# Two attention layers on one core: the order of every engine's steps read from a table instead of made by a list scheduler

## The reference

```python
# layer 0: 64 latents attend to 64 context rows and to themselves, 16 heads of 16
h = concatenate([ctx, x], axis=1)                       # (32, 128, 256)
q = x @ q_w + q_b;  k, v = split(h @ kv_w + kv_b)
attn = softmax(where(mask, q k^T / 16, -inf))            # 64 x 128 per head
r = (attn @ v) @ out_w + out_b + x
r = rmsnorm(r, postnorm_w)
x = gelu(r @ mlp_w1 + mlp_b1) @ mlp_w2 + mlp_b2 + x      # 256 -> 1024 -> 256
# layer 1: 256 columns attend to 256 columns of the context, 8 heads of 64
xn = (x - mean) * rsqrt(var + eps) * gamma + beta        # mean, var of a whole sequence
q = Wq xn + bq;  k, v = split(Wkv ctx + bkv)
att = softmax(q^T k / 8)                                 # 256 x 256 per head
out = x + Wo (att v) + bo
```

## Time and profile before

| | us |
|---|---|
| median of 3 runs | 603.48 |
| lowest, highest | 601.45, 603.9 |
| span of the profiled execution | 602.0 |
| PE busy | 570.4 |
| DVE busy | 547.9 |
| ACT busy | 504.4 |
| POOL busy | 420.8 |

### The profile page before, as it was taken

One profiled execution on the slowest core, in us unless ns is written; L12 is line 12 of the kernel. 1 busy time (PEld: TensorE's weight loads), 2 busy tenths in 40 slices (PEclk: granted clock), 3 DMA queues, 4 the chain that ended last, 5 costly groups with the idle time before them and its releaser, 6 DMA issues.

```text
span 602.0 us, 21122 instructions
## 1 busy us (share of the span) xinstructions
PE 570.4 (95%) x8564; PEld 463.7 (77%) x8564; DVE 547.9 (91%) x1053; ACT 504.4 (84%) x1904; POOL 420.8 (70%) x419
## 2 busy tenths in 40 slices
PE   4799999999999999999999999999999999998976
PEld 4689877777888787887888777887877777876755
DVE  5977889999999999999899989998999999999996
ACT  2848779988899987998899888998989897968873
POOL 2643468777588767796777865886676985787764
PEclk9779999999999999999999999999999999999989
DMA  8213001011102111111111111011111111110110
GB/s 285 76 38 103 22 19 55 20 37 30 35 29 57 43 38 28 38 56 32 33 46 55 38 38 27 31 35 29 37 29 38 32 38 40 37 29 20 40 24 23
DMA packets 50080, 26.45 MB, mean 44 GB/s; under 512 B 38048, under 2 KB 48320, under 8 KB 49984
## 3 DMA queue, kind: packets, MB, share of 16 engines
q1 hardware_dynamic: 49984, 25.11, 15.3%
HBM read 22.99 MB, written 2.10 MB: 42 GB/s over the span
## 4 chain that ended last, share of the span: by engine, by line
PE 64%; DVE 23%; ACT 6%; POOL 4%; DMA 2%; issue 1%; SPq 0%
PE bank L671 60%; DVE E1b L1179 6%; DVE nm L1162 5%; PE bank L792 4%; POOL E1b L1445 3%; ACT E1b L1362 3%; DVE nm L1017 2%; DVE E L1027 2%; DMA mski<-in_msk 1%; DVE QS L1155 1%; ACT E L1259 1%; DVE PT L1035 1%; DVE hm L1099 1%; ACT hm L1333 1%; DVE mrow L989 1%; PE bank L822 1%
## 5 line engine op out<-in xcount | busy, mean ns | idle before, releaser
L1445 POOL TENSOR_TENSOR E1b<-E1b,rs 128x512 f32<-128x512 f32 x255 | 264.0, 1060 | 85.4 <-DVE rs L1168 80.4
L1362 ACT ACTIVATE E1b<-bank,nm 128x256 f32<-128x256 f32 x512 | 237.0, 495 | 28.6 <-DVE nm L1162 28.4
L1162 DVE TENSOR_REDUCE nm<-bank 128x2 f32<-128x512 f32 x256 | 164.2, 674 | 9.4 <-PE bank L671 9.0
L1179 DVE STREAM_TRANSPOSE E1b<-E1b 128x1024 f32<-128x1024 f32 x128 | 155.9, 1227 | 5.7 <-POOL E1b L1445 4.8
L671 PE MATMUL bank<-ctx,QS 64*128 64x256 f32 x1024 | 134.5, 394 | 1.7 <-DVE PT L1035 1.0
L671 PE MATMUL bank<-E1b,CT 32*64 32x256 f32 (+1 forms) x4224 | 120.9, 375 | 10.2 <-ACT E1b L1362 3.6
L671 PEld LDWEIGHTS bank<-E1b,CT 32*64 32x64 f32 x4224 | 95.4, 132 | 30.4 <-ACT E1b L1362 5.1
L1362 ACT ACTIVATION_READ_ACCUMULATOR E1b<-bank,nm 128x1 f32 x512 | 116.7, 228 | 0.0
L671 PEld LDWEIGHTS bank<-ctx,QS 64*128 64x128 f32 x1024 | 91.6, 186 | 25.5 <-issue 6.8
L1259 ACT ACTIVATE E<-bank,nm 128x128 f32<-128x128 f32 x256 | 90.7, 409 | 9.6 <-DVE nm L1017 9.6
L1259 ACT ACTIVATION_READ_ACCUMULATOR E<-bank,nm 128x1 f32 x256 | 63.8, 249 | 0.0
(11 more groups left out here) (119 smaller groups left out, 823.1 us busy)
## 6 DMA issues: line engine op xcount, KB each, us to landing
CT<-in_hT SPq DMA_DIRECT2D x256, 32.0 KB, 1.9
hraw<-in_hT SPq DMA_DIRECT2D x8, 512.0 KB, 3.4
ctx<-in_ctx SPq DMA_DIRECT2D x32, 128.0 KB, 2.7
xnat<-in_xn SPq DMA_DIRECT2D x8, 256.0 KB, 2.8
E1b<-in_w SPq DMA_DIRECT2D x2, 1024.0 KB, 8.8
out<-y SPq DMA_DIRECT2D x16, 128.0 KB, 1.7
E1b<-in_kvw SPq DMA_DIRECT2D x2, 256.0 KB, 4.6
mski<-in_msk SPq DMA_DIRECT2D x32, 1.0 KB
```

Of the source, the lines that this page charges most:

```text
L1162: e.tensor_reduce(nm1[:, u % 16, :], bank[place["S", u]][:, :].rearrange("p (i t) -> p i t", i=2), AX.X, ALU.max, negate=True).then_inc(dv ...
L1179: e.transpose(E1b[:, k:k + 2, :, :], E1b[:, k:k + 2, :, :]).then_inc(dve_steps, 1)
L1362: t = e.activation(E1b[:, r, i, :], bank[bk][:, i * 256:(i + 1) * 256], ACT.Exp, bias=nm1[:, r, i:i + 1], scale=1.0, accum_out=sum1[:, r, ...
L1445: e.tensor_tensor(E1b[:, u % 16, :, :], E1b[:, u % 16, :, :], rs1[:, u % 16, :].unsqueeze(2).to_broadcast([128, 2, 256]), ALU.mult).then_i ...
```

## The change

`Plan.order()` no longer schedules. A table `ORDER` names for each of the five engines all of its steps in order, and for each PE step that takes banks the banks by number. `order()` reads the table, checks it against `plan()`, derives which step must have emptied a bank before its next use, and walks the lists into one order that respects all dependencies. `COST`, `SHIFT`, `MODE` and the due times are gone. The set of 2505 steps and their dependencies are the same. In the table some steps have another engine than before: of the 64 snp 13 run on DVE and 51 on POOL (22 and 42 before); ze 40 on DVE and 84 on ACT (47 and 77); W1e 18 and 14 (21 and 11); gs 21 and 11 (24 and 8); xn 5 and 11 (9 and 7); te 28 and 36 (27 and 37); Np none on DVE (one before); hhi 8 and none (6 and 2); a few of the weights' preparation the other way. One wait changes with it: q waits for xn and Mg on each engine where one of them runs, since they may now stand on two.

```diff
-ENTER = dict(rows=95, cols=92, rows32=95, cols32=95, grid=95)
-LEAVE = dict(rows=100, cols=162, rows32=100, cols32=140, grid=150)
...
-STAY = dict(full=0, rows=0.6, grid=2, cols=1.5, rows32=1.5, cols32=0)
...
+ORDER = {
...
+xol:1 qe:1:1 X:2 X:3 yy:1 sq:1 X:6 X:7 X:9 X:8 sn:2:0:2 X:1 X:0 sn:2:0:3 N:6 dd:1 X:5 rstd:1 te:2:0:2 X:4 te:2:0:3 N:2
...
     def order(self):
-        engines = ("PE", "DVE", "ACT", "POOL", "SP")
-        free = {e: 0 for e in engines}
-        mode, table = "full", "exp"
-        idle = [(0, b, None) for b in range(8)]
...
+        for step, banks in lists["PE"]:
+            assert len(banks) == len(self.banks[step])
+            for use, b in zip(self.banks[step], banks):
+                self.place[use], self.before[use] = int(b), holds.get(b)
+                holds[b] = self.emptied[use]
+        ahead, over = {e: 0 for e in lists}, set()
+        while len(self.steps) < len(self.todo):
...
                 elif name == "q":
                     p, c = key
                     pa, pb = take_all(("q", 2 * p, c), ("q", 2 * p + 1, c))
-                    w.wait_ge(*last([("xn", p), ("Mg",)]))
+                    for x in lasts([("xn", p), ("Mg",)]):
+                        w.wait_ge(*x)
```

More of the change, by code:

```diff
@@ L252, in order @@
-        self.span = max(over.values())
-        self.over = over
-        self.steps = [s for _, s in sorted(self.steps, key=lambda x: x[0])]
+        lists = {e: [(tuple(int(x) if x.isdigit() else x for x in word.partition("@")[0].split(":")),
+                      word.partition("@")[2]) for word in words.split()] for e, words in ORDER.items()}
+        for e, entries in lists.items():
+            for step, _ in entries:
+                assert e in self.on[step] and step not in self.runs
+                self.runs[step] = e
@@ new lines, in order @@
+        while len(self.steps) < len(self.todo):
+            n = len(self.steps)
+            for e, entries in lists.items():
+                while ahead[e] < len(entries):
+                    step = entries[ahead[e]][0]
+                    if not all(a in over for a in (*self.after[step], *(
+                            self.before[use] for use in self.banks[step] if self.before[use]))):
+                        break
+                    self.steps.append(step)
+                    over.add(step)
+                    ahead[e] += 1
+            assert len(self.steps) > n
@@ L315, in plan @@
                 prev("t", p2, r) for r in range(4)],
-                banks=[("s", g, c, r) for r in range(4)], kind="other")
+                banks=[("s", g, c, r) for r in range(4)])
             for r in range(4):
-                add("smax", g, c, r, on=A, at=at(), after=[("s", g, c), prev("t", p2, r)])
-                add("sexp", g, c, r, on=P, at=at(), after=[("smax", g, c, r), prev("t", p2, r)],
-                    empties=(("s", g, c, r), "other"))
-                add("sn", g, c, r, on=A, at=at(), after=[("sexp", g, c, r)])
@@ L357, in plan @@
+            add("W2", g, c, on=V, after=[("gsp", g, c), ("W2", g, c - 1) if c else None] + [
+                ("w2l", c)], banks=[("W2", g, 0)] if c == 0 else [])
+        add("X1", g, on=A, after=[("W2", g, 3), ("xop", g)] + (
+            [("fin", 2 * (g - 2) + i) for i in range(2)] if g >= 2 else []), empties=("W2", g, 0))
         if g + 1 < NG:
-            add("lx", g + 1, on=D, at=at(), after=[("X1", g)])
-    add("qs", on=A, at=HEADAT - 1, after=[("sm0",)])
-    add("obt", on=V, at=HEADAT + 8, after=[("wo0",), ("sm0",)], banks=[("obt",)], kind="other")
```

488 lines of the change are left out of this document (270 added, 218 removed), and 82 rows, old and new, of tables (COST, SHIFT).

## The result

| | before | changed |
|---|---|---|
| median, us | 602.94 (19 runs) | 601.13 (19 runs) |
| lowest, highest | 601.31, 605.99 | 598.84, 604.0 |
| span of the profiled execution | 602.0 | 598.1 |
| PE, DVE, ACT, POOL busy | 570.4, 547.9, 504.4, 420.8 | 562.3, 539.8, 506.2, 426.7 |

The ratio is 0.9966, 95% interval 0.9952 to 0.9979: 2 us faster where 11 were forecast, and within the 0.5% that I had called no change.

The account below looks back on a forecast made before the run. PE was taken as the bound from 107 to 555 us, three quarters of the run. -6.8 - 2.5 - 2.0 = -11.3 us from 602.0 gave 590.7, plus 1.5 for the median: 592.2 us, 1.9% less, range 584 to 602.5.

Parts of the forecast that it names:

- Part 2, the head: Up to 107 us: lighter DVE ahead of the split of group 0's output, -2.5 us, bounds -5 to +8.5.
- DVE gets lighter ahead of the split: Head, ahead of group 0's output split: four te go to ACT and one snp to POOL, 3.8 us off DVE.
- Rival 2: Head stays at 1.2 GHz longer, as s waits for four banks near 18 us: +8.5, 600.7 us; chance 0.08.
- shorter slow stretch: Head, 20 to 39 us at clock 0.55: -5 us was the bound if it and the waits shrink.
- Part 1, boundaries: 107 to 555 us: 59 fewer tile-shape changes on PE at 0.14 us each, -8.3 us.
- Part 1, new waits: 107 to 555 us: longer runs of one kind make some results later, 1.5 us of new PE waits.
- stays 15 us or more below: 107 to 555 us: DVE's work stays at least 15 us under the shortened time, so PE remains the bound.
- rival 3: Gain returns as waits at Z and Y: part 1 is 0 to -2, head or tail nothing, 601 us; chance 0.11.
- Part 3, the tail: After 555 us: DVE loses 3.2 us of work to ACT and POOL, -2 us, between -4 and +1.
- only what lies ahead of the last chain gets shorter: Tail: the chain from U through Zh, zh, Yh to fin is the same in both lists; -2 us for the tail.
- the +1 end of the range: Tail: ze later on ACT, and so Y later, +1 us.
- Rival 1: DVE runs dry in longer stretches without S, idle ahead of X above 30 us; 608, at worst 616 us; chance 0.08.

Follow-up runs that it names:

- its control: The kernel before with the same order and engines, only its PSUM banks handed out anew by the hybrids' simple rule: 603.49 us, ratio 1.0004.

## Why the prediction was wrong

The sum was -6.8 - 2.5 - 2.0 = -11.3 us. Traces that share an order give these lengths, with the head cut from the middle at the start of S 18:

| stretch | before's order | changed order | forecast | measured |
|---|---|---|---|---|
| head | 110.5 (108.8 to 112.0, 5 traces) | 112.3 (110.9 to 113.0, 5) | -2.5 | +1.8 |
| middle | 443.3 (3) | 438.8 (437.8 to 440.0, 4) | -6.8 | -4.5 |
| tail | 46.8 (before and its control) | 47.7 (47.3 to 48.1, first two) | -2.0 | +0.9 |

The runs with the shortened X are left out, and from the heads of before's order the two hybrids whose middle is the changed one: there S 16 stands ahead of the first Z, and S 18 starts 69.7 and 71.2 us after O. The three rows add up to -1.8, as much as the medians differ by. The head scatters by more than a microsecond from one execution to the next, so its +1.8 is known to about 1 us; its part behind O, +1.2, is known to 0.2.

- **Part 2, the head, failed most (4.3 us of 9.5).** The step that failed is "DVE gets lighter ahead of the split", with work counted at the durations that the trace of before shows. The new order puts the low part of wo and xop beside xo and xol, and there the two took 1.2 + 1.6 us in place of 0.4 + 0.7 for group 0. For group 1 xol has moved from POOL to DVE, and the two took 1.5 + 1.5 us, where DVE's part was 0.4 before. O waited 2.7 and 1.6 us. Taking the collision away gave 2.4 to 4.0 us by the medians, as much as was missing. I had read the move of xop in none of the excerpts, since POOL has room, and had not counted that of xol: of the steps that can stand on two engines, DVE also got two xol, two sq and an xo more.
- **Rival 2** named the head too, for the clock ahead of O, and that was not it: before's order has 6.8 to 17.1 us at 1.2 GHz there, the changed one 6.8 to 10.2. But with the wait at O goes a stretch of 3.4 us at 1.2 GHz that before's order does not have, so a part of the loss is the clock after all. The head of before with its 17.1 us at half clock was one of two such traces in eight; to hope for a shorter slow stretch was to forecast the luck of one execution.
- **Part 1, boundaries.** Right in kind and low in size: 59 at 0.18 (the whole middle) or 0.16 to 0.19 (measured alone), 10.6 us where I took 8.3.
- **Part 1, new waits.** I added 1.5 us; 6.5 came. PE's own idle time grew by just 1.5 (7.0 to 8.5), but waits under the end of a matmul do not show in it. That DVE "stays 15 us or more below" was right and beside the point: room on an engine is an average, and a step waits for one particular instruction. The halved X and E show that: 47 to 49 and 39 us of work less in the middle, 1 to 3 us less time. I had not looked at the banks, the resource that longer runs of S use up: 5.5 of 8 held before, 6.3 now. It was rival 3's way, with more than half of the gain lost and not all.
- **Part 3, the tail.** The step that failed is that only what lies ahead of the last chain gets shorter: the ze that left DVE for ACT now keep Y waiting for 2 us, the case that I had as the +1 end of the range. DVE's work did get less (39.3 us of busy time in the tail before, 38.5 now, one X and one U more among them), but that does not set this tail: with X over half of the columns DVE has 6 us less there and the tail is still 47.8 us. What the remaining difference to before's tail hangs on was not tested.
- **Rival 1** was wrong: 7.9 us of idle time ahead of X, under the 30 that I had set as its mark.

Shown by experiments are the price of a boundary, the collision in the head, that merging or reassigning alone loses 4%, and that waits taken out of PE's list bring nothing by themselves. That banks cause half of the returned 6.5 us is read from the timeline and supported by the shortened E; the small excesses are not explained. The tail's account is read from traces alone.

## What to carry over

Price a new order by its waits first: a merge is worth 0.18 us a boundary, one step put in front of what it needs costs 0.5 to 1.5. Count what a move takes of a shared resource, here PSUM banks held and the time that POOL and DVE run side by side, and not only each engine's busy time. Compare stretches of two orders between points ahead of which both have done the same steps. And do not forecast from a slow stretch at half clock in one profiled execution.

## What was not expected of the hardware

- A copy with rounding from SBUF to SBUF on DVE (128x512) took 0.43 us alone and 1.20 to 1.49 beside an instruction on POOL, a subtraction 0.69 and 1.5 to 1.64; POOL's addition took 1.45 and 1.54 beside them and 1.09 to 1.30 where xop was moved away. The Trainium skill ("SBUF — State Buffer", SBUF: two separate sides) says that the two engines share a pair of ports, and that of a POOL instruction and a DVE instruction with two inputs from SBUF (or in a mode that uses both ports) the one that starts first blocks the other for its whole length. The trace agrees: of the POOL instruction beside them 0.93 and 1.09 us were left when copy and subtraction of group 0 began, and they took 0.79 and 0.95 us longer than alone. That the copy, with one input, ran in such a mode is not shown.
- PE's clock fell to 1.2 GHz for 3.4 us at a wait of 1.8 to 2.7 us ahead of O of group 0 in nine traces of nine; in the ten traces in which O waited 0.7 us or not at all it did not fall there.
- A change of tile shape costs PE 0.186 us between 64\*128 and 128\*128 tiles, 0.162 between 64\*128 and 128\*64.
